# Two transformer layers on one core: attention heads regrouped over the tensor engine's strips, and one second-layer round moved forward in the order

## The reference, cut to what matters

```
# first layer, per sequence
h = ln(x) * (scale1 + 1) + shift1
q, k, v = split(h @ Wqkv.T + bias)
q = q / |q| * exp(min(scale_mul_log, log 100));  k = k / |k|
p = softmax(q @ k.T + mask);  x += (p @ v @ Wproj.T + bproj) * gamma1
h = ln(x) * (scale2 + 1) + shift2
x += (gelu(h @ Wfc1.T + bfc1) @ Wfc2.T + bfc2) * gamma2
second layer:
h = rms(x) * w1 * (1 + t @ tw1.T)
q, k = rope(h @ Wq.T), rope(h @ Wk.T);  v = h @ Wv.T
x += softmax(q @ k.T / sqrt(32)) @ v @ Wo.T
h = rms(x) * w2 * (1 + t @ tw2.T)
x += (silu(h @ Wg.T) * (h @ Wu.T)) @ Wd.T
```

## Time and profile before

| what | value |
|---|---|
| median of 3 runs | 386.43 us |
| lowest and highest run | 386.29 and 393.18 us |
| span of the profiled execution | 387.1 us |
| TensorE (PE) busy | 326.0 us, 84% |
| VectorE (DVE) busy | 256.0 us, 66% |
| ScalarE (ACT), GpSimd (POOL) busy | 199.8 us, 52%, each |
| mean granted TensorE clock | 0.907 of 2.4 GHz |

### The profile page before, as it was taken

The page is one execution under the profiler, slowest core; times in us unless marked ns, Lnnn a source line. Parts: engine busy times, 40 slices in busy tenths (PEclk is TensorE's granted clock), DMA queues, the critical chain, the costliest instruction groups (busy, mean ns, idle before and its releaser), DMA issues.

```text
span 387.1 us, 6924 instructions
## 1 busy us (share of the span) xinstructions
PE 326.0 (84%) x2240; PEld 262.6 (68%) x2240; DVE 256.0 (66%) x652; ACT 199.8 (52%) x681; POOL 199.8 (52%) x363
## 2 busy tenths in 40 slices
PE   4491575788868986998999999789999999998986
PEld 3261353466655875886776888567788888897975
DVE  3774889887889878657868785755864635434250
ACT  3234268657666688877645885643535525322110
POOL 6536958976687788258858655645522401302000
PEclk9985588576988996998999999969999999999999
DMA  7979130000000000002010000000000000000000
GB/s 219 215 242 322 56 128 10 27 2 1 1 2 1 2 3 1 2 2 54 3 55 0 2 3 1 3 0 0 2 1 3 14 15 0 15 14 2 28 2 27
DMA packets 14035, 14.27 MB, mean 37 GB/s; under 512 B 1568, under 2 KB 12960, under 8 KB 14000
## 3 DMA queue, kind: packets, MB, share of 16 engines
q1 hardware_dynamic: 14000, 13.83, 12.0%
HBM read 12.76 MB, written 1.06 MB: 36 GB/s over the span
## 4 chain that ended last, share of the span: by engine, by line
PE 61%; DVE 16%; POOL 10%; issue 6%; DMA 3%; SPq 2%; ACT 2%; DVEq 0%; POOLq 0%; ACTq 0%
PE ps_linear L1377 16%; PE ps_hidden L1200 7%; PE ps_output L1337 6%; PE ps_hidden L1202 5%; PE ps_hidden L1201 5%; PE ps_scores L1307 5%; PE ps_probs L1314 4%; PE ps_linear L1347 3%; DVE z L1115 2%; DVE qk_pack L1053 2%; DMA res_bias<-in_bfc 2%; PE ps_linear L1200 2%; PE ps_turn L1228 1%; DVE xn L978 1%; PE ps_linear L1202 1%
## 5 line engine op out<-in xcount | busy, mean ns | idle before, releaser
L733 POOL TENSOR_TENSOR z<-z,row_inv 128x512 f32<-128x512 f32 (+1 forms) x64 | 54.8, 859 | 61.8 <-DVE row_inv L1129 61.7
L836 ACT ACTIVATE z<-z,neg_max 128x128 f32<-128x128 f32 x128 | 49.6, 391 | 19.9 <-DVE neg_max L1118 19.8
L848 ACT ACTIVATE probsT<-ps_probs 128x512 f32<-128x512 f32 (+1 forms) x64 | 31.0, 485 | 35.3 <-PE ps_probs L1314 35.1
L1314 PE MATMUL ps_probs<-ident,z 128*128 128x128 f32 x192 | 36.6, 305 | 7.1 <-POOL z L733 6.3
L884 ACT ACTIVATE g_a<-ps_hidden 128x256 f32<-128x256 f32 x32 | 12.3, 384 | 45.7 <-PE ps_hidden L1202 45.5
L697 POOL TENSOR_TENSOR h_lo<-xn,h_hi 128x256 fp32r<-128x256 f32 x32 | 25.9, 812 | 18.0 <-ACT h_hi L799 17.8
L1314 PEld LDWEIGHTS ps_probs<-ident,z 128*128 128x128 f32 x192 | 25.5, 157 | 13.0 <-issue 9.6
L1377 PE MATMUL ps_linear<-Wfc2T,g_h 128*128 128x256 f32 x128 | 31.7, 404 | 1.0 <-DVE res_t L1142 0.8
L1377 PE MATMUL ps_linear<-WdT,g_h 128*128 128x256 f32 x128 | 29.4, 383 | 3.2 <-DVE g_h L1171 2.7
L839 ACT ACTIVATE z<-ps_scores,neg_max_s 128x128 f32<-128x128 f32 x64 | 23.0, 368 | 14.5 <-DVE neg_max_s L1123 14.4
L1377 PEld LDWEIGHTS ps_linear<-Wfc2T,g_h 128*128 128x128 f32 x128 | 25.1, 201 | 5.9 <-DVE res_t L1142 1.0
(11 more groups left out here) (150 smaller groups left out, 973.5 us busy)
## 6 DMA issues: line engine op xcount, KB each, us to landing
gamma<-gamma_scratch SPq DMA_DIRECT2D x8, 256.0 KB, 4.2
stage<-in_Wada SPq DMA_DIRECT2D x6, 256.0 KB, 7.2
X<-in_x SPq DMA_DIRECT2D x4, 256.0 KB, 6.9
stage<-in_Wqkv SPq DMA_DIRECT2D x4, 256.0 KB, 5.0
Wfc2T<-in_Wfc SPq DMA_DIRECT2D x1, 1024.0 KB, 11.0
stage<-in_Wfc SPq DMA_DIRECT2D x4, 256.0 KB, 6.2
WdT<-in_Wd SPq DMA_DIRECT2D x1, 1024.0 KB, 6.5
stage<-in_Wg SPq DMA_DIRECT2D x4, 256.0 KB, 2.7
```

Source lines behind the costliest of these rows:

```text
L733: pool.tensor_tensor(z[:, d, 0:U, :], z[:, d, 0:U, :], row_inv[:, d, 0:U].unsqueeze(2).to_broadcast([P, U, P]), ALU.mult).then_inc(probs_r ...
L836: ins = act.activation(z[:, d, u, :], z[:, d, u, :], ACT.Exp, bias=neg_max[:, d, u:u + 1], accum_out=total)
L848: act.activation(probsT[:, G % 2, 0:U, :], bank_of(key)[:, 0:U * P].rearrange("p (u q) -> p u q", u=U), ACT.Copy).then_inc(is_freed(key)[0 ...
L1314: ins = pe.transpose(bank[:, u * P:(u + 1) * P], z[:, G % DEEP, u, :], ident[:, :])
```

## The change

1. **Groups.** `GROUPS` now lists units. A first-layer sequence has four groups of four heads as before, but a `scores` step makes two groups at once (16 f16 products, two for each of eight heads; every second one works in the neighbouring 32 rows and writes the other of two banks). A second-layer sequence has two groups of four heads in place of four of two. Their scores go to two banks by turns in the same way. The two scores banks are one slot now: it is freed when both groups' mask additions are done, or in the second layer when exp of the unit is.
2. **Values.** The four heads of a group write four different strips of 32 output columns. The rows of Wproj and Wo are permuted on load to match.
3. **Softmax of the first layer.** `row_max` is split into `mask_add` and `row_max` (DVE). A new step `max_off` (POOL) subtracts the maximum, so exp is one activation over 128x512 without row sums. The probabilities are not divided. A second set of `values` products with a matrix of ones (`ones_pad`) gives the row sums in the other half of the output bank, and `attn_norm` (DVE) takes their reciprocal (128x256) and multiplies.
4. **Second layer.** The factor 1/sqrt(32) goes into Wq when that chunk is split, so the maximum is no longer scaled. The division stays on POOL.
5. **Other steps.** First-layer `norm_mod` moves from DVE to ACT. `gelu_poly` (POOL) goes: DVE's `gelu_inner` adds the constant itself and tanh's scale takes the rest.
6. **Order.** Pair 0's second layer becomes the fourth round, ahead of pair 3's first layer. Waits for an older user of a buffer name the last sequence of the same layer (`last_same`). All bases, offsets and some guessed durations are new, so every engine's list is new.

```diff
-ROUNDS = [(0, 0), (1, 0), (2, 0), (3, 0), (0, 1), (1, 1), (2, 1), (3, 1)]
+ROUNDS = [(0, 0), (1, 0), (2, 0), (0, 1), (3, 0), (1, 1), (2, 1), (3, 1)]
...
-ATT_BASE = [-163.5, -31.5, 33.5, 66.5, 63.0, 93.0, 88.0, 127.0]
+ATT_BASE = [-523.5, -67.5, 19.5, -19.0, -7.5, 82.0, 303.5, 3.5]
...
-              "scores": ["scores0", "scores1"], "probs": ["probs"], "output": ["output"]}
+              "scores": ["scores"], "probs": ["probs"], "output": ["output"]}
...
+GROUPS = [(n, u, b) for n in range(2 * len(ROUNDS)) for u in range(2) for b in range(2 - layer_of(n))]
...
+def heads_of(G):
+    n, u, b = GROUPS[G]
+    if layer_of(n) == 0:
+        return [4 * g + 2 * u + b for g in range(4)]
+    return [4 * g + 2 * u + c for c in range(2) for g in range(2)]
...
+            def max_off(G):
+                d = G % DEEP
+                pool.wait_ge(max_ready, G + 1)
+                pool.tensor_tensor(z[:, d, :, :], z[:, d, :, :], neg_max[:, d, :].unsqueeze(2).to_broadcast([P, 4, P]),
+                                   ALU.add).then_inc(max_taken, 1)
...
-            def gelu_poly(r, c):
...
+                if layer_of(GROUPS[G][0]) == 0:
+                    act.wait_ge(max_taken, group_ord(G) + 1)
+                    act.activation(z[:, d, :, :], z[:, d, :, :], ACT.Exp).then_inc(exp_ready, 1)
+                    return
...
+            def mask_add(G):
...
+                if b == 0:
+                    dve.wait_ge(*is_filled(key))
...
+                if b == 1:
+                    dve.wait_ge(mask_added, group_ord(G) + 1)
+                    dve.sem_inc(is_freed(key)[0], 1)
...
+            def attn_norm(n):
...
+                dve.reciprocal(o_inv[:, :], bank_of(key)[:, C:2 * C]).then_inc(sum_inverted, 1)
...
+                dve.tensor_tensor(o_full[:, n % 2, :, :].rearrange("p c q -> p (c q)"), bank_of(key)[:, 0:C],
+                                  o_inv[:, :], ALU.mult).then_inc(is_freed(key)[0], 1)
...
             def scores(U):
+                if layer_of(n) == 0:
+                    for g in range(4):
+                        for slab in (0, 2):
+                            for b in range(2):
+                                ins = pe.matmul(ps_scores[b][:, g * P:(g + 1) * P], qkT[rows[b], j, slab, g, :],
+                                                qkT[rows[b], j, 1, g, :], start=slab == 0, stop=slab == 2)
+                else:
+                    for g in range(2):
+                        for b in range(2):
+                            ins = pe.matmul(ps_scores[b][:, g * P:(g + 1) * P], qk1T[rows[b], j, g, :],
+                                            qk1T[rows[b], j, 2, :], start=True, stop=True)
...
             def values(G):
+                for part in range(2 - layer_of(n)):
+                    for k, h in enumerate(heads_of(G)):
+                        if layer_of(n) == 0:
+                            stat = ones_pad[:, e, :] if part else v_pad[:, j, h, :]
...
+                        at = part * C + u * P
+                        ins = pe.matmul(bank[QUAD * k:QUAD * (k + 1), at:at + P], stat, probsT[:, G % 2, k, :],
+                                        start=G == first and part == 0, stop=done, skip_group_check=True)
```

More of the change, by code:

```diff
@@ L270, in list_steps @@
+            add(("attn_copy", n), "DVE" if layer == 0 else "ACT", 0.75 if layer == 0 else 0.27, [("values", last), prev(("attn_copy",), n), prev(("project",), n, 2)],
+                frees=("values", first), at=g)
+            add(("project", n), "PE", 0.95, [("attn_copy", n), ("load_whole", "Wproj" if layer == 0 else "Wo"), prev(("project",), n)], "linear", at=g)
+            add(("residual", "a", n), "DVE", 0.335, [("project", n), prev(("residual", "a"), n)]
                 + ([("gamma_load", pair)] if layer == 0 else [])
@@ L676, in _ @@
             pool.memset(v_pad[:, :, :, :], 0.0)
+            for e in range(2):
+                for half in range(2):
+                    pool.memset(ones_pad[:, e, half * D0:(half + 1) * D0], 1.0 if half == e else 0.0)
             pool.memset(qk_bias[:, C:2 * C], 0.0)
```

388 lines of the change are left out of this document (198 added, 190 removed).

## The result

The changed kernel takes 355.8 us (median of 4 runs, 353.6 to 359.3), against 386.4 us before on the same chip (4 runs, 384.7 to 393.2). The ratio is 0.919, with a 95% interval of 0.912 to 0.926. The forecast was 348.5 us with a range of 331 to 370, and faster by over 2% with a chance of 0.93: the sign and the range held, and the forecast promised 7.3 us too much.

The account below looks back on a forecast made before the run. PE was taken as the bound from 180 to 360 us, and trips between engines, DVE fullest, from 60 to 180. 387.1 -21 -3 -8 -4 -5 +3 = 349.1, less 0.7 from span to median: 348.5 us, range 331 to 370.

Parts of the forecast that it names:

- PE is the bound from 180 us on, so PE work out is time out: From 180 to 360 us PE binds; regrouping second-layer scores and values there saves 21 us, each microsecond shortening the end.
- The order of the rounds: Pair 0's second layer, moved ahead of pair 3's first, partly fills empty PE time: -5 us, bounds 0 and -15.
- rival (4): The reordering gives nothing, gains are lost in waits, only second-layer PE work counts, partly given back: 381 us, chance 0.05.
- The reciprocal, taken at 0.84 with its product: First-layer reciprocal and product of 128x256 on DVE, eight times 0.84 us: 6.7 us, up to 14; 7 taken.
- rival (2): Column strips work two at a time and the reciprocal is slow: 368 us, chance 0.16.
- First-layer values, +2 with bounds 0 and +18: Sixteen value pieces instead of eight on PE: 0.63 us over four strips, 1.2 over two; +2 us taken.
- The shorter first-layer trip, -8: A first-layer group's trip between engines is 1.8 us shorter; together with DVE's relief worth 8 us.
- The start, -4: PE's idling before the first transpose of q and k shrinks: between 0 and -7 us, -4 taken.
- The shared scores slot, +3: One two-bank scores slot makes next scores wait for both mask additions or exp: +3 us, 0 to +12.
- rival (3): The shared scores slot decides and the kernel gets slower: 397 us in a mild form, chance 0.03.
- The step from span to time, -0.7: The profiled span stands 0.7 us above the median of the runs, so 349.1 becomes 348.5 us.
- PE over 95% busy in the last 120 us: A sign that the forecast is right: PE busy for over 95% of the last 120 us.

Follow-up runs that it names:

- old_table: The changed kernel's steps with the old order of rounds and all bases and offsets of the kernel before: 382.1 us, ratio 0.989 to the kernel before.
- old_round: The changed kernel with rounds in the old order, pair 0's second-layer attention due at 60 instead of -19, lists planned anew: 371.8 us, ratio 0.968.
- no_ones: The changed kernel without the first layer's products with the matrix of ones; the reciprocal reads the values' half of the bank: 356.5 us, ratio 0.925.
- start_loads: The changed kernel with only the whole loads of Wfc2, Wo and Wd put behind the first modulation chunks: 357.9 us, ratio 0.929.
- two_strips: The changed kernel with the values products of a group over two column strips instead of four: 362.2 us, ratio 0.941.

## Why the prediction was right or wrong

- **PE is the bound from 180 us on, so PE work out is time out: the work was right, the conclusion failed.** Scores came out as forecast (16 steps of 0.71, eight pieces; the tail is given back by 16 steps fewer of each kind, 32 in all and not 32 of each, and the forecast's -21 is worked out from 32), values at the good end (0.36 for eight pieces over four strips: 32 x 0.55 - 16 x 0.36 = 11.8 us of the 12 that I took). PE's busy time fell by 26.0 us in all. But old_table, with all of this work gone, is only 4.3 us faster. "A microsecond of PE work taken out is a microsecond off the end" held neither in old_table nor in old_round. As I read the waits, it holds only as long as PE's list has other work to do meanwhile: the pace of second-layer trips was just beneath PE's, and the in-order lists expose it. The larger units and their one slot may have their part in it.
- **The order of the rounds, forecast -5 with bounds 0 and -15: mis-sized.** It gave 16.0 us with the table made for it. I counted it as an extra on top of a gain that I took as safe. With the new table it is what turned the PE gain into time: pair 0's second layer gave the trips of both layers something to lie beside (my reading), and PE's busy share from 120 to 300 us is 91% (163.8 of 180) and not 83% (150.0) as in old_round. The 11 us more than forecast stand against the 20 that the PE terms lack on their own (21 and 3 forecast, 4.3 for all new steps together).
- **Tables as a term: missing.** I treated the new bases and offsets as the carrier of the order. With the new steps in place they are worth 10 us in the old order, 24 in the new. My rival (4), that the gains are lost in waits (381 us), is close to what old_table measured, 382.1: the mechanism showed there, and with the new table and order it did not.
- **The reciprocal, taken at 0.84 with its product: failed.** It is 1748 ns, with the product 2.17 us, 8 x 2.17 = 17.4 us where I took 7 and an upper bound of 14. The slope between the two small reciprocals (5 ns a column) gave 1.3 and was nearer than the row of the same shape that I chose. This is the sign of being wrong that the forecast had named (a reciprocal above 1 us), and half of rival (2). With this one cost taken out the kernel runs at 347.3 us (349 by the ratios), which is about as large as the whole miss; that the other errors cancel among themselves is luck. The Trainium skill (VectorE: DVE Perf Modes, First, the fixed hardware budget) has the reciprocal as an iterated divide with a repeat count of 8. Read as eight passes, my estimate from it was 3.4 us each: the direction was right, the number twice too high.
- **First-layer values, +2 with bounds 0 and +18: right at the low end.** The steps last no longer than before (0.57 against 0.56), and no_ones shows no cost of the ones. By the packing rule of the Trainium skill (TensorE: Matmul & The Clock Gate, Measured speedup vs the span model) a packed set lasts about as long as one product, which pointed to four strips side by side. The trace agrees: 0.57 us over four strips against 1.00 over two.
- **The shorter first-layer trip, -8: too large.** exp in four pieces gives back 3.3 us, not clearly told from nothing. There was little relief for DVE: 246.5 us where I had 235. What such relief is worth by itself stays open: 7.4 us less of reciprocals brought 5.7 to 8.5 us, 7.4 us less of copies nothing, with ACT's waits against it.
- **The start, -4: failed, 0.** The transpose came at 39.59 us, not near 36. The earlier roots did what I counted on for the pack (2.9 us earlier), but PE's list had put other work ahead of the transpose. I had named the whole loads ahead of the modulation chunks as the risk, and start_loads shows that moving them alone doesn't help; what I missed were that work in PE's list and `angles` on DVE, which wait 4.4 us for the last small load with the first norms and copy behind them. Moving loads, DVE's steps and ACT's pack together brings the transpose forward by 3.5 us (36.10), and the end by 2.8.
- **The shared scores slot, +3: about 2 in waits.** In the changed kernel PE's scores wait mainly for the copies of q and k (4.9 us in four places), and for the slot 1.4 us in three places (the mask additions) and 0.6 in one (exp). In the old order of rounds they do wait for it: 4.9 us in three places for exp. This is rival (3) in a mild form, where other work is short.
- **The step from span to time, -0.7: of no weight.** In each run here an execution's time is 1.8 us above its own span, so the profile before, at 387.1 us, seems to be that of an execution of about 389 us. Counted from the median before, the forecast's terms give 386.4 - 38 = 348.4 us, the same.
- **PE over 95% busy in the last 120 us: wrong.** It is 56.65 of 60 us and 51.28 of the last 57.4, 92% in all.

## What to carry to other kernels

With fixed in-order lists, the saving of work on the busiest engine is only an offer: ask which wait is just beneath it, and which other work stands in the list to cover that wait. A regrouping, the order of the rounds and the lists' priorities are one change, to be judged together: here they gave 4, 2 and 10 us or so one by one (the table and the order each on top of the new steps), and 31 together. Price an operation by its own rows, or by the slope of its own small cases, and not by another operation of the same shape; and where a bank is released only behind it, count its length as latency too.

## What the runs showed of the hardware that I had not expected

- A DVE reciprocal of 128x256 fp32 out of PSUM takes 1748 ns, where a product takes 425 and a copy 416; of 128x4, out of SBUF, 173 ns. The extra 252 columns cost 6.25 ns each.
- A 256 KB chunk issued right behind whole loads of 2.25 MB landed 9.8 us after its issue (start_loads); in the changed kernel, where they stand much earlier in the queue, it took 2.8 us.
- Fp32 pieces of 128x128 into four column strips run side by side (0.36 us for eight, 0.57 over two strips). Score pieces in two row strips against one take 0.54 against 0.99 us in f16 and 0.71 against 1.15 in fp32.
- Taking PE work out of a stretch with gaps can lower the granted clock: without the ones products 0.70 and not 0.82 from 60 to 120 us, with PE busy 47.3 us and not 45.3, and a mean clock of 0.893 to 0.908 over its four runs against 0.914 to 0.932 over those of the changed kernel. The other way round, two_strips has 8 us more of busy PE and the highest mean clock of all these profiled runs, 0.939 against 0.914.
